# Turning the row of maxima one unit earlier, releasing sums by bank, and moving expert weights and layernorms to other places of a fused cross-attention and mixture-of-experts kernel

## The reference

```
def _layernorm(x, axis=-1, eps=1e-05):
    m = jnp.mean(x, axis=axis, keepdims=True)
    v = jnp.var(x, axis=axis, keepdims=True)
    return (x - m) / jnp.sqrt(v + eps)
...
    q = (x @ w_q).reshape(B, Sq, HEADS, DIM_HEAD).transpose(0, 2, 1, 3)
    k = (context @ w_k).reshape(B, Skv, HEADS, DIM_HEAD).transpose(0, 2, 1, 3)
    v = (context @ w_v).reshape(B, Skv, HEADS, DIM_HEAD).transpose(0, 2, 1, 3)
    sim = jnp.einsum('bhid,bhjd->bhij', q, k) * SCALE
    attn = jax.nn.softmax(sim, axis=-1)
    out = jnp.einsum('bhij,bhjd->bhid', attn, v)
    return out @ w_o + b_o
...
    gate = jnp.einsum('td,edf->etf', h2, e_gate)
    up = jnp.einsum('td,edf->etf', h2, e_up)
    eout = jnp.einsum('etf,efd->etd', jax.nn.silu(gate) * up, e_down)
    spec = jnp.einsum('etd,te->td', eout, combine)
    return X + (shared + spec).reshape(B, S, d)
...
x = x + jnp.tanh(g_xattn[0]) * _L0_xattn_ref(_layernorm(x), ctx_768, ...)
x = x + jnp.tanh(g_ffn[0]) * _L0_ffn_ref(_layernorm(x), ...)
```

## Time and profile before

| | |
|---|---|
| median of 3 runs | 1334.48 us (1333.23 to 1334.59) |
| the profiled execution's own time | 1331.99 us |
| its span, first to last instruction | 1330.3 us |
| mean granted TensorE clock | 0.972 of full speed |
| busy: PE, DVE, ACT, POOL | 1246.8, 969.7, 821.9, 708.3 us |
| largest shares of the chain that ended last | PE 72%, DVE 10%, ACT 9%, issue 4%, DMA 3% |

### The profile page before, as it was taken

How to read it: one execution, slowest core, us unless ns; L and a number is a source line. 1 busy time by engine, 2 the same in 40 slices (tenths; PEclk the granted TensorE clock), 3 DMA queues, 4 the chain that set the end, 5 groups by cost and what they waited for, 6 DMA issues and landing times.

```text
span 1330.3 us, 34633 instructions
## 1 busy us (share of the span) xinstructions
PE 1246.8 (94%) x14472; PEld 910.8 (68%) x14472; DVE 969.7 (73%) x1762; ACT 821.9 (62%) x1476; POOL 708.3 (53%) x555
## 2 busy tenths in 40 slices
PE   6689699999999999999999999999999999889998
PEld 4356477777677776767676767777767676567776
DVE  6787486868686868686777777786868686956766
ACT  1336476766666666666666666676766666555664
POOL 3125356565655556465656556555555645544554
PEclk7789899999999999999999999999999999899999
DMA  6201603130303030303122120303030200000000
GB/s 170 65 1 23 176 14 79 14 80 13 80 14 73 14 78 9 78 16 69 25 36 57 30 63 13 80 14 80 14 80 14 63 14 16 13 16 1 8 8 13
DMA packets 122277, 57.27 MB, mean 43 GB/s; under 512 B 108262, under 2 KB 117706, under 8 KB 122122
## 3 DMA queue, kind: packets, MB, share of 16 engines
q1 hardware_dynamic: 122122, 55.07, 18.1%
HBM read 15.38 MB, written 0.82 MB: 12 GB/s over the span
## 4 chain that ended last, share of the span: by engine, by line
PE 72%; DVE 10%; ACT 9%; issue 4%; DMA 3%; POOL 1%; SPq 1%; DVEq 0%; ACTq 0%; POOLq 0%
PE psum L777 18%; PE psum L758 9%; PE psum L759 8%; PE psum L760 8%; PE psum L858 8%; PE psum L793 4%; PE psum L890 3%; PE psum L912 3%; PE psum L903 3%; DVE mx L1310 2%; DVE p_lo L449 2%; PE psum L805 2%; DMA qk_hi<-mrow 2%; ACT p L985 2%; ACT p_hi L986 2%
## 5 line engine op out<-in xcount | busy, mean ns | idle before, releaser
L449 POOL TENSOR_TENSOR p_lo<-p,p_hi 128x768 f16<-128x768 f32 (+1 forms) x144 | 295.8, 2058 | 296.5 <-ACT p_hi L986 182.7
L1310 DVE TENSOR_REDUCE mx<-psum 128x1 f32<-128x512 f32 (+1 forms) x585 | 364.0, 652 | 52.1 <-PE psum L858 45.7
L985 ACT ACTIVATE p<-psum 128x768 f32<-128x768 f32 (+1 forms) x256 | 214.9, 839 | 241.8 <-PE psum L760 235.3
L777 PEld LDWEIGHTS psum<-c_both,p_hi 128*128 128x128 f16 x4992 | 255.3, 98 | 65.6 <-issue 31.4
L777 PE MATMUL psum<-c_both,p_hi 128*128 128x97 f16 (+1 forms) x4992 | 280.5, 208 | 6.5 <-ACT acc_sb L1001 6.3
L758 PE MATMUL psum<-qk_hi,cT_both 97*128 97x384 f16 (+1 forms) x768 | 260.2, 339 | 17.7 <-DMA qk_hi<-mrow 11.0
L449 DVE TENSOR_TENSOR p_lo<-p,p_hi 128x768 f16<-128x768 f32 (+1 forms) x240 | 250.8, 1045 | 11.6 <-ACT p_hi L986 10.0
L759 PE MATMUL psum<-qk_lo,cT_both 96*128 96x384 f16 (+1 forms) x768 | 258.9, 337 | 0.0
L760 PE MATMUL psum<-qk_hi,cT_both 96*128 96x384 f16 (+1 forms) x768 | 256.7, 334 | 0.0
L858 PE MATMUL psum<-cT_both,qk_hi 96*128 96x512 f16 (+1 forms) x585 | 216.8, 371 | 21.0 <-issue 10.5
L990 ACT ACTIVATE p<-psum 128x384 f32<-128x384 f32 (+1 forms) x256 | 130.0, 508 | 143.6 <-PE psum L760 142.8
(11 more groups left out here) (201 smaller groups left out, 2111.5 us busy)
## 6 DMA issues: line engine op xcount, KB each, us to landing
c_both<-c_new SPq DMA_DIRECT2D x16, 768.0 KB, 3.9
ctx_nat<-in_ctx_dram SPq DMA_DIRECT2D x16, 528.0 KB
aT<-a_new SPq DMA_TRANSPOSE x64, 2.9
wg<-in_L_ffn_e_gate_dram SPq DMA_DIRECT2D x1, 1024.0 KB, 5.6
wu<-in_L_ffn_e_up_dram SPq DMA_DIRECT2D x1, 1024.0 KB, 8.1
wd<-in_L_ffn_e_down_dram SPq DMA_DIRECT2D x8, 128.0 KB, 5.8
out_dram<-x SPq DMA_DIRECT2D x4, 200.0 KB
x<-in_x_dram SPq DMA_DIRECT2D x1, 600.0 KB
```

Source lines behind the costliest of these rows:

```text
L449: engine.tensor_tensor(p_lo[0:m, i % 3, 0:w], p32[0:m, i % 3, 0:w], p_hi[0:m, i % 3, 0:w], ALU.subtract).then_inc(lo_made(b, i)[0], 1)
L777: t = mm(psum[:, ACCB + bank, k * (C + 1):k * (C + 1) + wide], p[0:m, i % 3, n * P:(n + 1) * P], c[parity][0:m, j, 0:wide], start=(j == 0 ...
L985: a(to32, src, ACT.Exp, scale=DH ** -0.5)
L1310: v.tensor_reduce(mx[:, rt, part:part + 1], bank[:, 0:w], AX.X, ALU.max)\
```

## The change

Four edits.

- The maxima are shared out over units 3 to 20 and m stands in unit 21. The shares by unit change thus: unit 7 has three maxima and not two, unit 9 one and not none, unit 10 three and not two, unit 21 none and not three. In middle batches f1 moves in unit 9 from the end of the unit to the place after the scores, since a maximum now has the end.
- `acc_out` counts each of the two copies of sums, and `pv_unit` waits for the copy of a bank just ahead of its first matmul into that bank, not for both ahead of the first.
- `load_experts()` is called in batch 1, after `turn(0, 1)`, and no longer ahead of it.
- The layernorms of groups 1 to 3 move from units 0 to 9 of batch 0 to units 7 to 15, and GpSimd's `token_rstd` from ahead of its loop to units 9, 11 and 13.

```
-    share = {i: 0 for i in range(3, 22)}
+    share = {i: 0 for i in range(3, 21)}
...
-    plan[22].append(("m", 0))
+    plan[21].append(("m", 0))
...
     for n in range(1, 4):
-        plan[2 * n - 2].append(("la", n))
-        plan[2 * n - 1].append(("lb", n))
-        plan[2 * n + 2].append(("lc", n))
-        plan[2 * n + 3].append(("x", n))
+        plan[2 * n + 5].append(("la", n))
+        plan[2 * n + 6].append(("lb", n))
+        plan[2 * n + 8].append(("lc", n))
+        plan[2 * n + 9].append(("x", n))
...
-            load_experts()
             for r in range((B - 4) // 2):
                 for b, kind, parity in ((r * 2 + 1, "odd", 1), (r * 2 + 2, "even", 0)):
                     ctx_made(b + 1, 1 - parity)
                     turn(b - 1, 1)
+                    if b == 1:
+                        load_experts()
                     turn(b, 0)
...
             def body(b, kind, parity):
                 if kind == "first":
                     ctx_lo(1, 1)
-                    token_rstd(1)
-                    token_rstd(2)
-                    token_rstd(3)
                 if kind != "first":
                     normalise(b - 1, 1)
                 for i in range(UNITS):
+                    if kind == "first" and i in (9, 11, 13):
+                        token_rstd((i - 7) // 2)
...
-                if j == 0 and not (isinstance(b, int) and b == 0 and i == 0):
-                    pe.wait_ge(acc_out, b * 2 + i // CH)
                 half = i // CH
                 for p, c, wide in ((p_hi, c_hi, C + 1), (p_hi, c_lo, C), (p_lo, c_hi, C + 1)):
...
                         bank, k = divmod(n, PER_BANK[half])
+                        if j == 0 and k == 0 and p is p_hi and c is c_hi and (b or half):
+                            pe.wait_ge(acc_out, (b * 2 + half - 1) * 2 + bank + 1)
...
                 for bank in range(2):
                     t0, t1 = bank * PER_BANK[half], min(TILES[half], (bank + 1) * PER_BANK[half])
-                    ins = a(acc_sb[:, t0:t1, :], psum[:, ACCB + bank, 0:(t1 - t0) * (C + 1)].rearrange(
-                        "p (k c) -> p k c", c=C + 1), ACT.Copy)
-                ins.then_inc(acc_out, 1)
+                    a(acc_sb[:, t0:t1, :], psum[:, ACCB + bank, 0:(t1 - t0) * (C + 1)].rearrange(
+                        "p (k c) -> p k c", c=C + 1), ACT.Copy).then_inc(acc_out, 1)
```

More of the change, by code:

```diff
@@ L211, in flamingo_kernel @@
     SET_DVE = [f"{n}0" for n in LN_A + LN_B] + ["wqT", "xln0", "Mh0hi", "Mh0", "xhi0", "xlnT0", "tn", "bot", "Mh1lo"] + \
-              [f"{n}{g}" for g, ns in ((1, LN_A), (1, LN_B), (2, LN_A), (2, LN_B), (1, ["xln"]), (3, LN_A), (1, ["xhi"]),
-                                       (3, LN_B), (2, ["xln"]), (2, ["xhi"]), (3, ["xln"]), (3, ["xhi"])) for n in ns] + \
-              ["Nh0", "Nh1", "Nh2", "x1 0", "Nh3", "x1 1", "x1 2", "x1 3"]
+              [f"{n}1" for n in LN_A + LN_B] + [f"{n}2" for n in LN_A] + ["xln1"] + [f"{n}2" for n in LN_B] + \
+              ["Nh0", "xhi1"] + [f"{n}3" for n in LN_A] + ["Nh1", "xln2"] + [f"{n}3" for n in LN_B] + \
+              ["Nh2", "xhi2", "x1 0", "Nh3", "xln3", "x1 1", "xhi3", "x1 2", "x1 3"]
     SET_ACT = ["wkT", "tx", "tf", "Mh1", "wvT"]
@@ L611, in normalise @@
                 hi, lo = (a_new[:, k, 0:n, 0:C] for k in range(2))
-                pool.wait_ge(acc_out, at + 1)
+                pool.wait_ge(acc_out, (at + 1) * 2)
                 g.tensor_tensor(acc_rc[:, 0:n], acc_sb[:, 0:n, C], minus_one[:, 0:n], ALU.pow).then_inc(acc_rcp, 1)
@@ L818, in aux @@
                     if n == 1:
-                        pe.wait_ge(acc_out, B * 2)
+                        pe.wait_ge(acc_out, B * 4)
                     if n == 3 * EU:
@@ L1375, in _ @@
             hi, lo = (a_new[:, k, 0:n, 0:C] for k in range(2))
-            dve.wait_ge(acc_out, at + 1)
+            dve.wait_ge(acc_out, (at + 1) * 2)
             v.reciprocal(acc_rc[:, 0:n], acc_sb[:, 0:n, C]).then_inc(acc_rcp, 1)
```

## The result

The changed kernel takes 1341.27 us (median of 5 runs, 1339.42 to 1345.55), the kernel before 1334.48 on the same chip: a ratio of 1.0049, 95% interval 1.0035 to 1.0064. It is slower by some 6.5 us; the prediction had 1322.5, in a range of 1312 to 1330, and gave slower a chance of 0.04.

The account below looks back on a forecast made before the run. The prediction took TensorE to bound a middle batch; from the profiled 1331.99 us, -12.0 (expert weights), +3.2 (row and sums) and -3.2 (layernorms) gave 1320.0, or 1322.5 on the median's scale, range 1312 to 1330.

Parts of the forecast that it names:

- Expert weights, -12.0: Batch 1: issuing the context transpose ahead of the expert weights' load removes TensorE's one-time loss, -12.0 us.
- the load's 11 us: Batch 1: SyncE's time for the moved expert load, some 11 us, said to be hidden by 19 us waits at turns.
- Row in unit 21, +0.35 a middle batch: Middle batches: moved maxima cost 0.61, a new wait 0.33; 0.05 and 0.54 come back, net +0.35 us each.
- The ring wait of unit 10: Unit 10: its second maximum needs f1's bank in a ring of three product banks, so TensorE waits 0.33 us.
- Sums by bank, -0.12 a batch: Unit 2: three matmuls go ahead once the first copy frees its bank, -0.12 us a batch, at most 0.45.
- Layernorms, -3.2: Batch 0: units 4 to 6 win 10.85 us, 8.2 go back, 2.7 stay; with 0.5 at the end, -3.2.
- over 81: Batch 0: a length over 81 us, against about 77.5 forecast, would show the prediction wrong.
- 42.1: Batch 0, units 7 to 16: VectorE's summed work after the layernorms' move, 42.1 us, making VectorE the bound.
- the second rival: Batch 0: moved layernorms collide with GpSimd at the shared SBUF port, up to +8.5 us, 1331.0; chance 0.08.
- the nine that it named: Batch 0: nine wide VectorE operations with two SBUF inputs, moved under GpSimd, each costing 0.94 us if hit.
- The one on the slower side: Batches' ends: TensorE's clock falls to 1.2 GHz, fourteen falls cost 31 us, 1353; chance 0.03.

Follow-up runs that it names:

- e3_bank: The kernel before with only the sums released bank by bank; 1344.26 us, ratio 1.0082.
- e4_norms: The kernel before with only the first batch's layernorms moved to units 7 to 15; 1337.18 us, ratio 1.0023.
- e1: The kernel before with only the expert weights' load moved into batch 1; 1321.84 us, ratio 0.9915.
- e2: The kernel before with only the row turned in unit 21 and the maxima in units 3 to 20; 1335.66 us, ratio 1.0017.
- e6: The changed kernel without the sums by bank, the other three parts kept; 1330.90 us, ratio 0.9975 to the kernel before.
- e8_shift: The changed kernel with GpSimd's residue of unit 4 waiting for GpSimd's own division, no order against VectorE; 1326.55 us, ratio 0.9946.
- e5: The changed kernel with one wait more: GpSimd's residue of unit 4 begins only behind VectorE's residue of unit 3; 1324.85 us.
- e10_late: The kernel before with VectorE's residue of unit 3 in middle batches waiting for VectorE's own last maximum; 1347.88 us, ratio 1.0106.

## Why the prediction was wrong

**Expert weights, -12.0: right.** Batch 1 fell by 10.63 in the changed kernel, where it has the middle batches' loss too, and by 11.9 where the load was moved alone. SyncE issues batch 1's transpose at 133.70, 0.71 before the first scores, and the load's 11 us were covered as the prediction said.

**Row in unit 21, +0.35 a middle batch: right.** +0.28 alone. The ring wait of unit 10 came (7.2 us in 14 waits, 0.51 each, for 0.33 worked out), and the batch's last three units and the next first one gave back 0.5.

**Sums by bank, -0.12 a batch: this is the step that failed.** The gain itself is there, 0.20. Unit 2 of batch 7 by windows, in the kernel before and in e3_bank:

```profile
561.15:564.06 2.91, 2.46 (x40) 1.79 (x38) 1.43 (x2) 2.85 (x7) 1.38 (x1) 1.00 1.22 366
```

```profile
568.76:571.47 2.71, 2.56 (x41) 1.82 (x38) 1.44 (x2) 2.71 (x7) 1.18 (x1) 1.00 1.22 342
```

What was wrong is the bound: "a loss is excluded as far as an extra wait of TensorE costs under 0.05". That looked at the engines which the edit touches, TensorE and ScalarE. It did not ask what 0.2 us mean for the distance between those engines and GpSimd, whose division and residue of unit 4 run against VectorE's residues of units 2 and 3. The edit alone made VectorE the loser of that collision in nearly every batch: 1.13 us each. Over 14 batches that is 15.8 us, and it turns the forecast's -12.0 into a loss, together with the next term. The term came out at +0.93 a batch (1.13 less 0.20) and not at -0.12: 14.7 of the 18.8 us between the forecast and the measurement.

**Layernorms, -3.2: wrong in sign, by its size.** Batch 0 became 2.4 us longer, 83.13; over 81 stood among the prediction's own signs of being wrong. Units 4 to 6 fell to 9.07, and where the residues are in order to 8.15, the very figure forecast: the collision of the two residues lengthens unit 5 of batch 0 as well. But from unit 7 to 17, 47.29 us passed and not 42.1. VectorE is the bound there as predicted (busy 44.52 of 47.29, had 30.91 of 33.98); the sum of its work was short. Its groups in that stretch:

```profile
L1309 DVE TENSOR_REDUCE mx<-psum 128x1 f32<-128x512 f32 (+1 forms) x20 | 12.7, 652 | 2.0 <-PE psum L858 1.7
L449 DVE TENSOR_TENSOR p_lo<-p,p_hi 128x768 f16<-128x768 f32 (+1 forms) x7 | 8.1, 1158 | 0.0
L1268 DVE TENSOR_TENSOR x<-x,bot 100x512 f32<-100x512 f32 x4 | 4.8, 1199 | 0.0
```

The four bias sums take 4.8 where 2.8 were booked (two of them were held to 1.62 and 1.81), the residues 8.1 for 7.6, there are 20 maxima and not 19, and the two small operations of each layernorm, left out, are some 1.7 together. VectorE stood idle for the other 2.8 us of the stretch, most of it before maxima that TensorE had not made yet. And TensorE, waiting for VectorE, had a mean granted clock of 0.82 in that stretch against 0.96, so it ran at 1.2 and not 2.4 GHz for a larger part of it. So the second rival happened in part, to other operations than the nine that it named. Its price, 8.5, was too high, the forecast's zero too low.

**The rivals.** The one on the slower side had the clock fall at the batches' ends; the granted clock is 1.00 in the middle batches, and a batch's end won as forecast. The port was weighed for batch 0 alone. The trace of before held the sign of it: two GpSimd residues in 4.43 us that take 1.64 each alone, in each middle batch, beside a VectorE residue of 0.94. A collision whose price an idle engine pays looks free, and it was not on the list of what could turn.

**What decides the order, and what stays open.** The distance is 0.38 us both in the kernel before, where VectorE goes first, and after, where it doesn't; it differs by no more than some 10 ns from batch to batch. At 0.26 VectorE goes first in 13 batches of 14, at 0.49 in none of 13. So the distance matters, but at 0.38 something else tells the two cases apart. What the sums by bank move is what stands ahead: the last pass of GpSimd's division (L621, L622 in the changed kernel) begins 0.26 before VectorE's residue of unit 2 in the kernel before, 0.05 before it after. In both it ends 2.23 behind that residue's start, so it takes 2.49 before and 2.28 after. The single batches that fall out of line do so in this too. In e3_bank, batch 10 (VectorE held) and batch 11 (VectorE first):

```profile
784.43 2.29 POOL L621 TENSOR_TENSOR a_new<-acc_sb,a_new 128x672 f16<-128x672 f32 x1
...
854.14 2.44 POOL L621 TENSOR_TENSOR a_new<-acc_sb,a_new 128x672 f16<-128x672 f32 x1
```

In e4_norms, batch 10, the one where VectorE is held:

```profile
778.52 2.19 POOL L621 TENSOR_TENSOR a_new<-acc_sb,a_new 128x672 f16<-128x672 f32 x1
```

It holds throughout. The kernels before and after, e1, e2, e3, e4 and e6 have this pair at 0.37 to 0.38 in 94 batches: in 66 of them that pass took 2.44 to 2.52 us and VectorE went first, in the other 28 it took 1.98 to 2.31 and GpSimd did, without an exception. In e8_shift, at 0.26, it took 2.28 to 2.31 where VectorE went first, and 1.99 in batch 10, where GpSimd did. So the order goes with the length of that pass, which the sums by bank shorten. That is read from all the traces; no run moved the pass alone, so that its length is what turns the order isn't shown, and why it should isn't known. Batch 10 of several kernels has it short because GpSimd begins the division's second pass 0.3 us late, and why it does so is open. Open too is a second pair, VectorE's residue of unit 11, 0.08 behind GpSimd's of unit 12: in the changed kernel, e5, e6 and e8 it takes 0.95 in the middle batches, and some 2.5 in batch 10 alone.

## What to carry to other kernels

Before a small edit on a tuned kernel is booked at its own gain, look in the trace for pairs of instructions that already hold each other up, also where an idle engine pays: an edit that moves one of them by a tenth of a microsecond can hand the bill to the engine that everybody waits for, in every turn of the loop. Where the order of such a pair matters, write it down as a wait (here one wait was worth 16 us) and don't leave it to the timing. And when work is moved under an engine that is then the bound, add up all of its operations there, the small ones and the hits too: it was a sum of 42 that came to 47.

## What the runs showed of the hardware

A VectorE subtraction with both inputs in SBUF (128x768) takes 0.94 us alone and 1.88 to 2.20 when GpSimd's residue of this size is served first; GpSimd's takes 1.64 alone and 2.68 to 2.83 when it begins 0.24 to 0.38 ahead and VectorE's is first. The loser goes on when the other is about done: VectorE's, 0.38 behind and 1.13 longer, behaves as if held until 1.51 of GpSimd's 1.64 had passed.

Who goes first is not simply who begins first in the records. GpSimd began 0.26 us (e8_shift) and 0.38 us (kernel before) ahead and VectorE was served first; 0.49 ahead (e10_late) and GpSimd was. At 0.38 either was, and it went with the length of GpSimd's instruction before, in 94 batches of 94: VectorE first where that took 2.44 to 2.52 us, GpSimd where it took 1.98 to 2.31. The Trainium skill, SBUF — State Buffer, section "Who interferes with whom", says that issue order decides who blocks: by that, GpSimd would have gone first in all of these. The measurement differs, as far as the records' begin is the issue; whether it is, no run here shows.
